# GpSimd's indirect DMAs on a ring of two semaphores instead of six, in a kernel of two expert layers around a token mixer

## What is computed

```python
x = x + 0.5 * ffn(layernorm(x), Wg, Wup, bup, Wdown, bdown)
x = x + attn(layernorm(x), ...)
x = x + 0.5 * ffn(layernorm(x), Wg, Wup, bup, Wdown, bdown)

# ffn: 12 experts, each token takes its best 3
topw, sel = top_k(x @ Wg, 3)
cw = softmax(topw) placed at sel
h = gelu(x @ Wup[e] + bup[e])          # 128 -> 512
y = h @ Wdown[e] + bdown[e]            # 512 -> 128
out = sum over e of cw[e] * y[e]

# attn: gated projection, a causal recurrence over the tokens with one factor per channel,
# a normalisation, a gated projection and two output projections
```

## Time and profile before

| | before |
|---|---|
| time, median of 3 runs | 853.14 us (850.62 to 855.24) |
| time of the profiled execution | 848.97 us |
| its span, first to last instruction | 846.9 us |
| granted TensorE clock, mean over the span | 0.873 |
| indirect DMAs | 407 |

### The profile page before, as it was taken

One profiled execution on the slowest core, in us unless ns is written; L12 is line 12 of the kernel. 1 busy time (PEld: TensorE's weight loads), 2 busy tenths in 40 slices (PEclk: granted clock), 3 DMA queues, 4 the chain that ended last, 5 costly groups with the idle time before them and its releaser, 6 DMA issues. The chain is left out here.

```text
span 846.9 us, 17502 instructions
## 1 busy us (share of the span) xinstructions
PE 639.4 (76%) x4525; PEld 580.4 (69%) x4525; DVE 375.0 (44%) x1735; ACT 514.1 (61%) x1465; POOL 414.2 (49%) x424
## 2 busy tenths in 40 slices
PE   7678669788877789876762888955847778898896
PEld 5467569687867677765661777844746668888894
DVE  8654756320102467754351447844441552222224
ACT  4474545676755588763641678934634656667685
POOL 1444364566555461334446665135344655666552
PEclk9998788899986899967885799968757999999999
DMA  9941312223423232111221322211113332132243
GB/s 244 248 141 44 98 59 58 76 78 110 126 72 88 54 91 60 47 36 60 76 79 46 91 78 79 60 51 40 39 46 90 87 105 64 52 96 74 62 174 100
DMA packets 98984, 71.50 MB, mean 84 GB/s; under 512 B 13504, under 2 KB 91894, under 8 KB 98890
## 3 DMA queue, kind: packets, MB, share of 16 engines
q1 hardware_dynamic: 82890, 42.84, 18.4%
q0 software_dynamic: 13024, 26.11, 10.8%
q10 hardware_dynamic: 2976, 1.44, 0.6%
HBM read 36.30 MB, written 34.75 MB: 84 GB/s over the span
## 5 line engine op out<-in xcount | busy, mean ns | idle before, releaser
L1213 ACT ACTIVATE hT<-ps,BU 128x128 f32<-128x128 f32 x900 | 259.8, 388 | 202.1 <-remote 92.5
L1026 PE MATMUL ps<-xT,WT 128*128 128x128 f32 x1800 | 274.9, 300 | 69.5 <-issue 34.1
L1039 PE MATMUL ps<-WD,hT 128*128 x1800 | 274.3, 298 | 59.2 <-issue 42.1
L1026 PEld LDWEIGHTS ps<-xT,WT 128*128 128x128 f32 x1800 | 249.6, 213 | 85.9 <-issue 84.0
L1039 PEld LDWEIGHTS ps<-WD,hT 128*128 128x128 f32 x1800 | 247.9, 212 | 71.3 <-issue 70.9
L2066 DVE TENSOR_TENSOR Ys<-ps,BD 128x128 f32<-128x128 f32 x225 | 64.0, 288 | 374.0 <-PE ps L1039 209.8
L806 POOL DMA_INDIRECT xs<-XN,SX x144 | 145.2, 1008 | 171.2 <-issue 110.6
L824 POOL DMA_INDIRECT YG<-ys,SY x132 | 134.9, 1022 | 85.8 <-issue 45.3
L1092 ACT ACTIVATE WT<-WU 128x512 f32 x225 | 149.6, 666 | 8.1 <-PE ps L1026 2.9
L836 POOL DMA_INDIRECT yk<-Ys,row x71 | 70.8, 997 | 63.8 <-DVE Ys L2066 37.9
L1186 ACT ACTIVATE xT<-ps 128x512 f32<-128x512 f32 (+1 forms) x52 | 31.8, 611 | 45.4 <-remote 38.2
(11 more groups left out here) (369 smaller groups left out, 604.0 us busy)
## 6 DMA issues: line engine op xcount, KB each, us to landing
ys<-Ys SPq DMA_DIRECT2D x41, 256.0 KB
xl<-xs SPq DMA_DIRECT2D x94, 64.0 KB
xl<-xs SPq DMA_DIRECT2D x71, 66.0 KB
WU<-in_L_ffn_Wup_dram SPq DMA_DIRECT2D x12, 256.0 KB, 5.0
WD<-in_L_ffn_Wdown_dram SPq DMA_DIRECT2D x12, 256.0 KB
YG<-yk SPq DMA_DIRECT2D x4, 768.0 KB, 6.0
xs<-XN,SX POOLq DMA_INDIRECT x144
YG<-ys,SY POOLq DMA_INDIRECT x132
```

What stands on the lines that cost most here:

```text
L1026: x = e.matmul(HB[i % 2][:, c * P:(c + 1) * P], WT[i % NW][:, c, :], xT[m % 2][:, j * P:(j + 1) * P], start=True, stop=True)
L1039: x = e.matmul(YB[i % 2][:, 0:D], hT[i % 3][:, c * P:(c + 1) * P], WDf[:, bass.ds(r + c * P, P)], start=(c == 0), stop=(c == C - 1))
L1213: x = e.activation(hT[i % 3][:, c * P:(c + 1) * P], HB[i % 2][:, c * P:(c + 1) * P], ACT.Gelu, bias=BU[:, bass.ds(b + c, 1)])
```

## The change

```diff
-AIR = 6
+AIR = 2
```

## The result

| | before | after |
|---|---|---|
| time, median of the runs | 854.17 us (4 runs, 850.62 to 855.24) | 770.37 us (4 runs, 769.64 to 771.84) |
| ratio after to before, 95% interval | | 0.9028 [0.8996, 0.906] |
| span of the profiled execution | 846.9 us | 767.7 us |
| granted TensorE clock, mean | 0.873 | 0.911 |

The four runs of the kernel before are the three behind the forecast's 853.14 us and one more.

The account below looks back on a forecast made before the run. PE's matmuls and ACT's gelu were taken to bound the kernel, POOL having room. First tiles 0, phases 0 to 2 0, phase 3 0, tail +0.4, removed waits -0.2 gave +0.2 us: 853.3 us, range 849.3 to 857.4.

Parts of the forecast that it names:

- What bounds the kernel now: Opening step: PE's matmuls and ACT's gelu make the chain; POOL, 49% busy, has room; six DMAs in flight never limit.
- Rival 4: Something unseen in the work's order shifts PE's waits or granted clock: 848.9 or 857.4 us, chance 0.04.
- The round trip: POOL's indirect DMAs, from issue until POOL can act on the landing: 2.42 us a scatter, 2.83 us a gather.
- A stream of scatters isn't slowed: POOL's scatter streams: a round trip of 2.42 us fits under 2.57 us, with 0.15 us to spare.
- First tiles: Tiles 2 and 3, while the weights load: a late gather costs 0, at worst 0.4 us.
- The removed waits: Semaphore waits dropped on ACT, PE, DVE and SP: 0.2 us saved, 1.7 us if all ACT's and PE's count.
- The tail: Last scatters, issued into four loads of 768 KB: +0.4 us, between nothing and 1.6 us.
- rival 2: Phase 3: two slots are too few, 1.78 us a step against 1.67, 11.7 us more, 865 us; chance 0.08.

Follow-up runs that it names:

- ring of one: One semaphore where the kernel before had six, so each indirect DMA waits for the landing of the previous one: 1318.71 us, ratio 1.549.

## Why the prediction was wrong

**The step that failed** is in "What bounds the kernel now": "So the first question is not how many DMAs POOL can have under way but whether a wait for the second one back comes later than POOL would have issued anyway." It took POOL's issues as free for everybody else, and the rest follows from that: "What stands behind a late DMA on POOL is only the next DMA". A wait on POOL could then only cost, and in the sum what it gives back to TensorE stands at nothing, without a reason. The runs showed that closely spaced issues delay TensorE's completions by up to 25 us, and that pauses between them are worth 80 us and more; the change gave back 84.3 us in phases 0 to 2. The evidence was there: part 4 of the page gave 6% of the chain to "another core or an unknown queue" on a kernel with one core, which is 50 us of the 319 us that the chain covers. The second line of the earlier trace rows ends with 11.5 us of "remote", and the 4.13 us that PE sat for ACT in the earlier trace rows are one more case (ACT's copy at 47.93 us waited for "remote"). The stretch of the earlier trace rows was read on POOL alone; ACT's wait of 15.15 us stood beside it. The earlier trace rows were read as the whole kernel, but that chain begins at 524.64 us, so they say nothing of phases 0 and 1. The share of busy time misled as well: PE was busy 76% in the earlier trace rows, but in the stream from 434 to 465 us 13.17 us of 31.

**Rival 4** ("something I don't see in the order of the work") had the right place, PE's waits and its clock, and no mechanism; its size, a few us, was short by 75.

**The round trip** was right in its typical size and short in its spread. In the ring of one, where every landing is on record, the median is 2.3 us for a scatter and 2.6 for a gather, counted from the start of the issue; forecast were 2.14 and 2.55. "A stream of scatters isn't slowed" rested on a round trip of 2.42 us, 0.15 us under the step of two; at 2.3 us nothing is left of that. In the long stream of the changed kernel 36 scatters start from 505.12 to 559.86 us, 1.56 a step where 1.29 was forecast. One piece of POOL's timeline:

```profile
521.36 0.98 POOL L806 DMA_INDIRECT xs<-XN,SX  x1 [0.80 <-DMA xs<-XN,SX]
522.64 0.98 POOL L806 DMA_INDIRECT xs<-XN,SX  x1 [0.30 <-issue]
525.85 0.98 POOL L806 DMA_INDIRECT xs<-XN,SX  x1 [2.23 <-DMA xs<-XN,SX]
527.13 0.98 POOL L806 DMA_INDIRECT xs<-XN,SX  x1 [0.30 <-issue]
```

The median step is 1.29, as forecast, but single landings are slow: the scatter at 525.85 starts 4.49 us after the one whose landing it waits for (521.36), where 2.42 was forecast. The two landings of the earlier trace rows were typical ones, and two slots wait for the slow ones. Gathers: 17 from 415.26 to 442.22 us, 1.69 a step, beyond the 1.30 to 1.64 given; one wait of 1.46 us for PE's pace is in it. These lengthened steps are the pauses that let TensorE go on.

**First tiles** came out at no cost, but not by the argument: the first matmul of line 1026 starts at 37.8 us, 38.8 before, and the 4.13 us of PE behind ACT in the earlier trace rows shrink to 2.08. **The removed waits** (-0.2) held in so far as they are worth nothing that can be seen: with six semaphores kept, the gain is the same.

**The tail** was mis-sized: +0.4 us, at most 1.6, by the prediction. PE's last matmul of line 1039 ended 16.7 us before the end of the span; after, 29.4, so it costs 12.7. The chain of the changed kernel there, and PE's and POOL's last rows:

```profile
730.30 6.22 DMA yk<-Ys,row
...
741.32 4.90 issue
...
753.75 2.12 DMA yk<-Ys,row
...
756.02 4.79 DMA WD<-yk
```

```profile
735.46 2.88 PE L1039 MATMUL ps<-WD,hT 128*128 x24
```

```profile
740.95 4.97 POOL L836 DMA_INDIRECT yk<-Ys,row  x1 [1.39 <-DMA yk<-Ys,row]
...
753.75 0.98 POOL L836 DMA_INDIRECT yk<-Ys,row  x1 [0.63 <-issue]
```

The place was right: a scatter issued into the four loads of 768 KB takes 6.22 us to land, and one issue lasts 4.97 us. But the prediction let DVE release the last pairs every 3.5 us, with time to catch up. With TensorE no longer held, PE is done at 738.34 and POOL's last scatter starts 15.4 us behind it, 1.4 before. So **rival 2** had the right place, phase 3, and by luck the size: 1.73 us a step (106 steps from 569.95 to 753.75), close to the 1.78 it was priced at. Its reason, a landing that counts only from the end of the issue, is not what the ring of one shows. The 12.7 us of the tail are hidden by 92 us gained elsewhere.

The Trainium skill (SBUF — State Buffer, "Who interferes with whom") lists one contended port pair, that of GpSimd and VectorE, and says that DMA never contends with a compute engine. Here TensorE is held under POOL's indirect DMAs by up to 25 us, and the measurement decides.

## What to carry to other kernels

On one core, a wait that the profile puts down to "remote" or to an unknown queue is a question to be answered before anything is priced: lay the timelines of the waiting engine, of its producer and of POOL over the same stretch. Where GpSimd issues indirect DMAs in long streams beside matmuls, try a pause ahead of every second one in those stretches alone; here it was worth 12.0% throughout and 13.6% without phase 3, more than a limit on what is under way (9.7 to 10.2%). Drop the pause where POOL is already late, above all at the end, where it cost 7.0 us here.

## What the runs showed of the hardware

Back-to-back indirect DMAs on POOL, 1.00 us each and 0.30 apart, delay TensorE's completions by up to 25 us, and PE then goes on one or two matmuls at a time, 1.4 to 2.1 us apart. ACT's and DVE's signals are not late (95 of 100 within 0.02 us). A gap of 0.9 us after each DMA removes the lateness, after every second one nearly (90th percentile 0.69 us), after every third only in part (2.85), and gaps of 0.41 us hardly (3.10, where the kernel before has 3.50). Half the bytes of the gathers change nothing (ratio 1.0013). While PE is held its clock falls too, a little later: 0.67 of full speed was granted from 434 to 465 us, 0.93 in the same kind of stream with the pauses (376 to 397). What POOL's indirect DMAs and TensorE's completions have in common no run here can tell; it stays open.
